# A ring of 41 buffer slots, one scratch tile and an earlier gamma product in a one-core graph kernel

## What is computed

```python
# layer 0
u = par_u[0] * par_u[1] * (diag_u[:, None] * ego_u @ W_u) + ego_u   # 2048 users
i = par_i[0] * par_i[1] * (diag_i[:, None] * ego_i @ W_i) + ego_i   # 3072 items
e = concatenate([u, i])
h = adj @ (adj.T @ e)
l0 = (h - mean(h)) * rsqrt(var(h) + 1e-5) * ln_gamma + ln_beta + x
x = layernorm(x + l0)
# layer 1: two rounds of message passing over the edges whose softmax score
# reaches a threshold; where no edge reaches it, every message is zero
x = layernorm(x + message_layers(x, adj, ...))
```

## Time and profile before

| | us |
|---|---|
| median of 3 runs | 394.97 |
| lowest and highest | 394.34, 395.02 |
| profiled execution | 394.63 |
| span of its core | 392.6 |
| TensorE busy in it | 377.1 (96%) |
| VectorE busy | 322.2 (82%) |
| ScalarE busy | 269.8 (69%) |
| moved from HBM | 107.6 MB, 277 GB/s over the span |

### The profile page before, as it was taken

How to read it: one execution, slowest core, us unless ns; L and a number is a source line. 1 busy time by engine, 2 the same in 40 slices (tenths; PEclk the granted TensorE clock), 3 DMA queues, 4 the chain that set the end, 5 groups by cost and what they waited for, 6 DMA issues and landing times.

```text
span 392.6 us, 13661 instructions
## 1 busy us (share of the span) xinstructions
PE 377.1 (96%) x5922; PEld 227.8 (58%) x5922; DVE 322.2 (82%) x309; ACT 269.8 (69%) x527; POOL 65.5 (17%) x130
## 2 busy tenths in 40 slices
PE   8969999999999999999999999999999999999990
PEld 7957564664476556546654654565466456555770
DVE  3889999999579969778886978797698869795674
ACT  3887798599099998587867748785786868501143
POOL 2020200300030300110030003003000300277375
PEclk9999999999999999999999999999999999999996
DMA  8999999999992799579778957987795799400012
GB/s 268 350 349 336 390 386 385 385 385 386 385 386 64 268 378 387 197 267 369 280 270 322 387 196 269 392 318 261 272 386 184 279 360 386 159 3 2 23 35 86
DMA packets 62112, 109.84 MB, mean 280 GB/s; under 512 B 3808, under 2 KB 14816, under 8 KB 62048
## 3 DMA queue, kind: packets, MB, share of 16 engines
q1 hardware_dynamic: 61760, 108.84, 77.6%
q10 hardware_dynamic: 288, 0.09, 0.1%
HBM read 107.60 MB, written 1.31 MB: 277 GB/s over the span
## 4 chain that ended last, share of the span: by engine, by line
PE 90%; SPq 4%; DMA 3%; DVE 1%; POOL 1%; issue 0%; POOLq 0%; ACT 0%
PE quad L1522 45%; PE quad L1502 43%; SPq L1038 3%; DMA pooled<-in_adj 3%; PE quad L1537 2%; DVE pooled L1290 1%; POOL pooled L1117 1%; SPq L1024 1%; POOLq L96 0%; POOL pooled L1112 0%; DVE pooled L1368 0%; DVE pooled L1408 0%; ACT pooled L1188 0%; PE quad L1577 0%
## 5 line engine op out<-in xcount | busy, mean ns | idle before, releaser
L1270 DVE STREAM_TRANSPOSE pooled<-pooled 128x1024 f32<-128x1024 f32 x200 | 230.1, 1209 | 2.5 <-ACT scratch L1158 2.4
L1158 ACT ACTIVATE scratch<-pooled 128x1024 bf16<-128x1024 f32 x200 | 210.1, 1052 | 32.1 <-DMA pooled<-in_adj 30.0
L1502 PE MATMUL quad<-pooled,rows_in 128*64 128x256 f32 (+1 forms) x1760 | 179.5, 361 | 3.0 <-DMA pooled<-in_adj 3.0
L1522 PE MATMUL quad<-pooled,col_sum 32*64 32x512 f32 (+4 forms) x3968 | 178.6, 507 | 0.4 <-DVE pooled L1290 0.2
L1502 PEld LDWEIGHTS quad<-pooled,rows_in 128*64 128x64 f32 x1760 | 120.6, 137 | 65.8 <-issue 15.1
L1522 PEld LDWEIGHTS quad<-pooled,col_sum 32*64 32x64 f32 x3968 | 87.6, 132 | 81.9 <-issue 63.3
L1290 DVE TENSOR_TENSOR pooled<-pooled,quad 128x2048 f32<-128x2048 f32 (+5 forms) x32 | 58.1, 1816 | 40.4 <-PE quad L1522 40.2
L1089 POOL COPY col_sum<-col_half 32x256 f32<-32x256 f32 (+1 forms) x88 | 33.2, 378 | 307.6 <-DVE col_half L1279 304.2
L1167 ACT COPY col_sum<-col_half 32x256 f32<-32x256 f32 (+1 forms) x88 | 33.7, 383 | 45.1 <-DVE col_half L1279 44.0
L1158 ACT ACTIVATION_READ_ACCUMULATOR scratch<-pooled 128x1 f32 x200 | 37.6, 188 | 0.0
L1188 ACT ACTIVATE pooled<-quad 128x256 f32<-128x256 f32 (+2 forms) x7 | 3.3, 476 | 23.4 <-PE quad L1537 23.4
(11 more groups left out here) (45 smaller groups left out, 60.0 us busy)
## 6 DMA issues: line engine op xcount, KB each, us to landing
pooled<-in_adj SPq DMA_DIRECT2D x200, 512.0 KB, 9.3
pooled<-in_x SPq DMA_DIRECT2D x5, 256.0 KB, 4.0
pooled<-in_x SPq DMA_DIRECT2D x1, 768.0 KB, 5.3
pooled<-in_x SPq DMA_DIRECT2D x1, 512.0 KB, 3.8
out<-pooled SPq DMA_DIRECT2D x2, 256.0 KB, 2.2
out<-pooled SPq DMA_DIRECT2D x2, 192.0 KB, 1.9
out<-pooled SPq DMA_DIRECT2D x3, 128.0 KB, 2.2
pooled<-in_w_ui ACTq DMA_DIRECT2D x1, 64.0 KB, 3.3
```

Source lines behind the costliest of these rows:

```text
L1158: nc.scalar.activation(scratch[v % 2][:, :], slots[slot_of(v)], ACT.Square, accum_out=square_sum[:, v:v + 1]).then_inc(unit_scanned, 1)
L1270: nc.vector.transpose(tiles, tiles).then_inc(unit_turned, 1)
L1502: mm = pe.matmul(block_bank(c)[half(h), 0:w // 2], rows_in[:, t, :], slots[slot_of(v)][:, at:at + w // 2], start=(t == 0), stop=(t == T - 1))
L1522: mm = pe.matmul(round_banks(g)[a][half(b % 2), 0:w].rearrange("p (t r) -> p t r", r=32), col_sum[c % 2][quadrant(a), b, :], to[quadrant(a ...
```

## The change

It does four things. (1) Slots become a ring of 41: unit v lies in slot (9 + v) mod 41 and so follows unit v - 41. A round must read its units from one straight stretch, so in blocks 4, 6 and 8, which the ring's end cuts, the parts are made to end there: (10, 16, 14), (12, 16, 12) and (14, 16, 10) tiles in place of (10, 14, 16). (2) `scratch` is one tile, and `scan(v)` waits until scan v - 1 has ended (before: v - 2). (3) The two small matrices of gamma's product lie in the last columns of `h_sum`; so the product must be done before block 0's last round is added there. `make_gamma_and_beta`, the product on TensorE and add 2 change places for that. (4) The tiles of the end lie in other slots (`X_SLOT` 5), and the wait for `e_made` stands at the first load into slot 0, now unit 32.

The memory freed by (2) and (3) is what slot 41 takes.

```diff
-    SLOTS = 40
-    SLOT_FIRST = [20, 30] + [0 if c % 2 == 0 else 20 for c in range(2, NB)]
+    SLOTS = 41
+    SLOT_FIRST = [(9 + UNIT_FIRST[c]) % SLOTS for c in range(NB)]
...
     PARTS = [((0, 8), (8, 16), (24, 16))] * 2 + [((0, 10), (10, 14), (24, 16))] * (NB - 3)
+    PARTS[4] = ((0, 10), (10, 16), (26, 14))
+    PARTS[6] = ((0, 12), (12, 16), (28, 12))
+    PARTS[8] = ((0, 14), (14, 16), (30, 10))
...
-        X_SLOT = 20
+        X_SLOT = 5
...
-        scratch = [sb(f"scratch{k}", [P, SLOT], bf16) for k in range(2)]
+        scratch = sb("scratch", [P, SLOT], bf16)
...
-        center_t = sb("center_t", [D, P])
-        center_g = sb("center_g", [D, D])
+        center_t = h_sum[0:D, N - P:N]
+        center_g = h_sum[0:D, N - P - D:N - P]
...
-            return SLOT_FIRST[c] + i
+            return (SLOT_FIRST[c] + i) % SLOTS
...
-                    assert SLOT_FIRST[2] == 0 and SETUP_SLOTS <= UPB[2]
+                if v < UNIT_FIRST[3] and slot_of(v) == 0:
+                    assert c == 2 and i + SETUP_SLOTS <= UPB[2]
                     sp.wait_ge(e_made, LGROUPS)
...
                 wait_loaded(act, v)
-                if v >= 2:
-                    act.wait_ge(unit_scanned, v - 1)
-                nc.scalar.activation(scratch[v % 2][:, :], slots[slot_of(v)], ACT.Square,
+                if v:
+                    act.wait_ge(unit_scanned, v)
+                nc.scalar.activation(scratch[:, :], slots[slot_of(v)], ACT.Square,
                                      accum_out=square_sum[:, v:v + 1]).then_inc(unit_scanned, 1)
...
-            add_round(2)
             first = UNIT_FIRST[2]
             make_gamma_and_beta()
-            for v in range(first, first + 4):
+            for v in range(first, first + 2):
+                turn_unit(v)
+            dve.wait_ge(gamma_turned, 1)
+            add_round(2)
+            for v in range(first + 2, first + 4):
                 turn_unit(v)
...
-            for v in range(first, first + 7):
+            multiply_unit(first)
+            pe.wait_ge(gamma_made, 1)
+            pe.matmul(bank[3][:, 0:D], center_t[:, :], center_g[:, :], start=True, stop=True).then_inc(gamma_turned, 1)
+            for v in range(first + 1, first + 7):
                 multiply_unit(v)
             multiply_round(3)
-            pe.wait_ge(gamma_made, 1)
-            pe.matmul(bank[3][:, 0:D], center_t[:, :], center_g[:, :], start=True, stop=True).then_inc(gamma_turned, 1)
```

More of the change, by code:

```diff
@@ L41, in adjacency_layers_kernel @@
     UNITS = UNIT_FIRST[NB]
-    SLOTS = 40
-    SLOT_FIRST = [20, 30] + [0 if c % 2 == 0 else 20 for c in range(2, NB)]
+    SLOTS = 41
+    SLOT_FIRST = [(9 + UNIT_FIRST[c]) % SLOTS for c in range(NB)]
     assert sum(WIDTHS) == N and max(WIDTHS) == CH
     PARTS = [((0, 8), (8, 16), (24, 16))] * 2 + [((0, 10), (10, 14), (24, 16))] * (NB - 3)
+    PARTS[4] = ((0, 10), (10, 16), (26, 14))
+    PARTS[6] = ((0, 12), (12, 16), (28, 12))
+    PARTS[8] = ((0, 14), (14, 16), (30, 10))
     PARTS += [((0, 12), (12, 12), (24, 8), (32, 8))]
+    assert all((SLOT_FIRST[c] + t // UNIT_TILES[c]) % SLOTS + nt // UNIT_TILES[c] <= SLOTS
+               for c in range(NB) for t, nt in PARTS[c])
     ORDER = [(c,) + part for c in range(NB - 1) for part in PARTS[c]]
@@ L158, in adjacency_layers_kernel @@
         minus_half = sb("minus_half", [P, GT])
-        piece_at = [N * i for i in range(4)] + [ln_at + N * i for i in range(4)]
+        piece_at = [0] + [ln_at + N * i for i in range(7)]
         piece = [pooled[:, a:a + N] for a in piece_at]
-        assert 4 * N <= x_at and piece_at[-1] + N <= POOLED
+        assert N <= x_at and piece_at[-1] + N <= POOLED
         ring, turned, carved_from, rest = piece[0:4], piece[4:6], piece[6], piece[7]
@@ L420, in turned_of @@
             w = WIDTHS[c]
-            at = SLOT * SLOT_FIRST[c] + w * first
+            at = SLOT * slot_of(UNIT_FIRST[c] + first // UNIT_TILES[c])
             return pooled[:, at:at + w * nt].rearrange("p (t b r) -> p t b r", b=w // 32, t=nt)
```

## The result

The changed kernel takes 397.38 us (median of 7 runs, 397.01 to 398.33), the kernel before 394.97 (7 runs). The ratio is 1.0065, with a 95% interval of 1.0052 to 1.0077: slower by 2.4 us, three times what was forecast, and 0.4 over the range. (The ratio is not the quotient of the two medians; here and in the experiments the two differ by up to 0.1%, less than the width of its interval.) The profiled execution took 397.19, which is 2.56 over the profiled execution before; its span is 394.9, 2.3 over the span before. The other 0.3 us lie outside the span.

What follows compares the result with a forecast made beforehand. TensorE, busy 377.1 of 392.6 us, was taken as the bound. Gamma's 0.1 plus 0.72 for one scratch made 0.8 us, on the median 394.97 giving 395.8; range 394.9 to 397.0.

Steps and rivals of the forecast that it cites:

- One scratch: ScalarE's scans of ready units: period 1.19 in place of 1.04, delaying TensorE's round B of block 3 by 0.72 us.
- the place at block 3: Seam of 0.12 us on TensorE ahead of round B, released by VectorE's addition, no slack left; forecast +0.72.
- the formula: At block 3, VectorE's last turn before its addition starts twelve scan periods after 113.27: 12 x 1.19 gives 127.55.
- the hand-off within ScalarE: Wait from one scan's end to the next start: taken as 0.03 us, between 0 and 0.10.
- The second seam: TensorE ahead of round B of block 2: free to go at 88.76, wanted at 88.79, so covered by 0.03 us.
- The hand-off is slow, and a second seam opens: Rival, from scan period 1.20 on: round B of blocks 2 and 3 both late, 396.0 to 397.1 us; chance 0.26.
- Gamma: Product moved up on TensorE, VectorE's addition behind the turns of units 20 and 21: cost 0.1 us ahead of round 3.
- Ring: Loads come up to one unit, 1.35 us, earlier; TensorE waits for no load after 26.03, so 0.
- Parts: Uneven splits in blocks 4, 6, 8 keep three rounds of 40 tiles in all, at the same cost: 0.

Runs made afterwards that it cites:

- e7: Kernel before, two scratches, but scans of units 61 to 79 wait for the scan just ahead: 396.12 us against 395.00, ratio 1.0021.
- e9: Changed kernel with a single scan, unit 60's, ahead of ScalarE's copies for block 3: 396.31 us against 395.08 for the kernel before, ratio 1.0024.
- e2: Changed kernel with two 1-byte scratch tiles and the wait for the scan before the last: 395.35 us against 394.87 for the kernel before, ratio 1.0012.
- e5: Kernel before with gamma's move alone: 395.36 us against 395.00, ratio 1.0011.
- e8: Changed kernel with two 1-byte scratches and scans ahead of the copies of blocks 2 and 3: 394.93 us against 395.00 for the kernel before, ratio 0.9992.
- e1: Kernel before with one scratch tile and the wait for the scan just ahead, nothing else: 397.57 us against 394.87, ratio 1.0059.
- e3: Changed kernel, ScalarE scanning 3 and 8 units ahead of its copies for blocks 2 and 3: 395.41 us against 394.87 for the kernel before, ratio 1.0020.
- e4: Kernel before, ScalarE scanning 3 and 8 units ahead of its copies for blocks 2 and 3: 394.74 us against 394.87, ratio 0.9996.
- e6: Kernel before, two scratches, but scans of units 2 to 19 wait for the scan just ahead: 395.01 us against 395.00, ratio 0.9997.
- e10: Kernel before, two scratches, but scans of units 41 to 59 wait for the scan just ahead: 395.41 us against 395.08, ratio 1.0002.

## Why the prediction was wrong

- **One scratch: the mechanism, the place at block 3 and the formula were right, one duration was not.** The step that failed is the hand-off within ScalarE, for which I took 0.03 from VectorE's wait for itself. ScalarE's is 0.09 (113.98 to 114.07). The period is then 1.24, and 12 x 0.05 = 0.6 us more come at block 3: 1.37 measured, 0.72 forecast. e7 and e9 show that this period, and nothing else of the change, sets that seam. I had the other row beside it, 0.10 from ScalarE to VectorE, and should have taken ScalarE's own signal for the better guide, whoever waits for it.
- **The second seam: forecast covered by 0.03, measured 0.55.** By my own formula a period of 1.24 gives 0.33. The rest is the 0.19 of unit 47: I read that no load is waited for after 26.03 from rows that merge many instructions. That wait held TensorE back and so lent cover to add 6, 0.46 in place of 0.27 us; it was there by chance (4 of the 12 profiled executions have it), and in that of the changed kernel it fell away. To the time it adds nothing: the seam is 0.19 longer, the row ahead of it 0.19 shorter.
- **The rival came true.** "The hand-off is slow, and a second seam opens", from a period of 1.20 on, was given 0.26; at 1.24 its terms are 0.1 + 0.33 + 1.32 = 1.75, 396.7, inside the range. (The 0.15 given for the second seam at 1.22 should be 0.18; the sum of 1.3 stays.) The time lies over 397.0 because two terms were in no case, gamma's break (0.15) and what lies outside the span (0.3); whether the 0.3 at the head and the end belong to the change is open.
- **Gamma: 0.1 forecast, 0.28 measured.** 0.15 of it is a term I had left out, the break in the row of units; the other 0.12 to 0.13 is the wait for add 2, which stands behind the turns of units 20 and 21, whose scans start 1.24 apart. With two scratches (e2, e5) only the 0.15 is left.
- **Ring: 0, right.** 210.76 to 210.78 in all kernels, and e8. Loads do come earlier: with two scratches ScalarE's waits for them fell from 30.0 to 25.7 us (e2), with TensorE none the faster. The 10.4 of the changed kernel is in good part something else, scans that take longer and so wait less (20.6 in e1, without the ring).
- **Parts: 0, right.** The block with (14, 16, 10) runs from 285.32 to 320.44 us, 35.12, as every other. No seam opened behind round B of block 3.
- **What the 2.56 us between the two profiled executions are.** From unit 20 to the last rounds the rows give 0.28 (gamma) + 0.55 + 1.37 (seams) = 2.20, less the 0.19 at unit 47 that fell away, 2.01. Another 0.18 was already there at unit 20 (44.55 against 44.37), 0.1 lies behind 342.50, and 0.3 outside the span.
- **Outside the span: in no term, 0.3 measured.** In the runs of every kernel with gamma's move (changed, e2, e3, e5, e8, e9) the execution is 2.3 us longer than the span (medians 2.29 to 2.33); in the kernel before and those without the move (e1, e4, e6, e7, e10) 2.0 to 2.1 (medians 1.98 to 2.09). e5 shows that it comes with gamma's move alone. The cause stays open. It is most of the 0.5 and 0.4 by which e2 and e5 are over the kernel before. Of the 0.54 of e3, whose TensorE takes 295.85 from unit 20 to the last rounds, 0.09 less than before, some 0.3 stay open.
- **The head is not settled to the tenth.** The arrival at unit 20 varied from 43.9 to 46.1 us over the profiled executions. The two latest, e1 and e9 (46.06), had TensorE at a granted clock of 0.66 between 26 and 31 us, where all others had 1.00. The changed kernel waits 0.83 for ScalarE's late copies ahead of round A of block 0, yet that round is over at the same time as in e5, with two scratches, where GpSimd's copies held it (next row of TensorE at 29.15 and 29.14, unit 20 at 44.55 and 44.54). e6 gives the scans of the head -0.9 to +0.6 us by its interval. So a few tenths there can be neither shown nor excluded.

The Trainium skill's page on ScalarE (ScalarE: Activation LUTs, What ACT_TABLE_LOAD costs) has neighbouring ACTIVATEs overlap by about 93 ns. No overlap of that size can be read from the rows here: with two scratches scans start 1.04 to 1.06 apart at 1.04 to 1.06 us each, and the read of 0.19, beside the next ACTIVATE, costs nothing. What the wait takes away is 0.20, not 0.09, because the read is then in the way as well. The Trainium skill's page on VectorE (VectorE: DVE Perf Modes, The DRAIN you can't avoid) finds for eight copies on VectorE that a semaphore after each costs nothing. That does not carry over to ScalarE's scans: waiting for the one just ahead made each 0.20 us longer.

## What to carry to other kernels

A buffer that is only written still has a price when it is made single: it ties each instruction to the end of the one before, and an engine that looks a third idle (69% busy) may be at its limit in the stretch behind a block of other work. Price it there, at the one place where no cover is left, and take the hand-off from rows of the same engine's signals; where a hundredth of a microsecond is paid twelve times over, as here, forecast the worse end. Look for waits in weight loads and in row lengths per unit, not only in brackets, since merged rows swallow them, and in more than one execution, since such a wait may be there in one and not in the next. Compare the whole execution with its span, too: 0.3 us of this change stood in no row. And before memory is bought for more load-ahead, ask who waits for loads: a ring one slot longer gave TensorE nothing.

## What the runs showed of the hardware

- A scan with an accumulator read, 128 x 1024, repeats every 1.04 us when each waits only for the one before the last, and every 1.24 when it waits for the last: 0.96 to the read, 0.19 for the read, 0.09 until the next starts (changed kernel, 112.83 to 114.07; with two scratches and the wait alone, e7, 113.56 to 114.80).
- The same hand-off within VectorE took 0.03 us (8.22 to 8.25).
- An output of one byte per number made the ACTIVATE no faster and no slower than bf16 (1.04 to 1.06, e2).
- A small matmul with another shape, put between two units on TensorE, cost 0.15 us beyond the 0.36 that it took between a round and a unit (e2, e5).
- The granted clock of TensorE was 0.66 between 26 and 31 us in two profiled executions (e1, e9) and 1.00 in the ten others; round A of block 0 took 2.95 us there (e1, 27.79) in place of 1.98.
